# Sliced feed-forward on one core: the softmax over slices by sample halves, and half of the weight transposes moved

## What is computed

```python
fx_mid = (x @ W_fx + b_fx).reshape(B, N, H, D).transpose(0, 2, 1, 3)
x_mid = (x @ W_x + b_x).reshape(B, N, H, D).transpose(0, 2, 1, 3)
slice_weights = softmax((x_mid @ W_slice + b_slice) / temp, axis=-1)
slice_norm = slice_weights.sum(axis=2)
slice_token = einsum('bhnc,bhng->bhgc', fx_mid, slice_weights)
slice_token = slice_token / (slice_norm[..., None] + 1e-05)
q, k, v = slice_token @ W_q, slice_token @ W_k, slice_token @ W_v
attn = softmax(einsum('bhgc,bhkc->bhgk', q, k) * SCALE, axis=-1)
out_slice = einsum('bhgk,bhkc->bhgc', attn, v)
out_x = einsum('bhgc,bhng->bhnc', out_slice, slice_weights)
out_x.transpose(0, 2, 1, 3).reshape(B, N, INNER) @ W_out + b_out
```

## Time and profile before

| | us |
|---|---|
| median of 3 runs | 1218.9 |
| the runs | 1215.72, 1218.9, 1219.8 |
| the profiled execution | 1216.68 |
| its span | 1214.8 |
| mean granted TensorE clock | 0.977 of full speed |

### The profile page before, as it was taken

How to read it: one execution, slowest core, us unless ns; L and a number is a source line. 1 busy time by engine, 2 the same in 40 slices (tenths; PEclk the granted TensorE clock), 3 DMA queues, 4 the chain that set the end, 5 groups by cost and what they waited for, 6 DMA issues and landing times.

```text
span 1214.8 us, 43735 instructions
## 1 busy us (share of the span) xinstructions
PE 1131.3 (93%) x16184; PEld 787.9 (65%) x16184; DVE 856.7 (71%) x3021; ACT 752.9 (62%) x2435; POOL 617.1 (51%) x939
## 2 busy tenths in 40 slices
PE   6988979999999789999999997999999999999997
PEld 3447845555555467887788786777777764566765
DVE  5974679999999868787877775555555555766664
ACT  0126779999999745555555554566666666655453
POOL 6012568888888644555556554233333332345545
PEclk9988999999999999999999998999999999899999
DMA  7000000000000000000000000000000000000000
GB/s 239 1 1 1 3 2 1 0 0 0 0 0 0 2 2 3 0 0 0 0 0 0 0 1 2 2 0 0 0 0 0 0 1 1 1 11 11 17 17 19
DMA packets 10835, 10.26 MB, mean 8 GB/s; under 512 B 9233, under 2 KB 9873, under 8 KB 10641
## 3 DMA queue, kind: packets, MB, share of 16 engines
q1 hardware_dynamic: 10768, 9.35, 2.6%
HBM read 7.25 MB, written 2.10 MB: 8 GB/s over the span
## 4 chain that ended last, share of the span: by engine, by line
PE 65%; ACT 21%; DVE 6%; issue 5%; POOL 2%; DMA 0%; SPq 0%; ACTq 0%; POOLq 0%; DVEq 0%
ACT big L787 13%; PE bank L1473 8%; PE bank L1807 5%; PE bank L1155 5%; PE bank L1825 5%; PE bank L1468 5%; PE bank L1144 3%; PE bank L1456 3%; PE bank L1233 3%; PE bank L159 3%; PE bank L1164 3%; PE bank L1182 2%; PE bank L1586 2%; PE bank L1223 2%; PE bank L1203 2%
## 5 line engine op out<-in xcount | busy, mean ns | idle before, releaser
L787 ACT ACTIVATE big<-big 128x128 f32<-128x128 f32 x512 | 218.1, 645 | 0.5 <-DVE big L836 0.5
L787 ACT ACTIVATION_READ_ACCUMULATOR big<-big 128x1 f32 x512 | 181.5, 444 | 0.0
L620 POOL TENSOR_TENSOR big<-big 128x512 f32<-128x512 f32 x128 | 133.0, 1040 | 47.8 <-DVE big L825 47.6
L1058 POOL TENSOR_TENSOR big<-big 128x512 f32<-128x512 f32 x64 | 65.5, 1045 | 126.9 <-DVE big L1332 126.9
L1554 POOL TENSOR_TENSOR big<-g_a,g_b 64x64 f32 x128 | 40.1, 313 | 171.8 <-DVE g_a L1544 171.8
L836 DVE CUSTOM_DVE_ANT_0 big<-bank,cst 128x128 f32<-128x128 f32 x512 | 117.9, 287 | 2.3 <-issue 2.3
L1535 DVE TENSOR_TENSOR_SCAN g_t<-g_zero_r,bank 128x128 f32<-128x128 f32 x128 | 53.9, 421 | 87.0 <-ACT g_zero_r L1520 87.0
L738 PEld LDWEIGHTS bank<-cst,big 128*128 128x128 f32 x512 | 55.7, 141 | 68.9 <-POOL big L620 25.0
L1520 ACT ACTIVATE g_zero_r<-bank,g_bias 128x64 f32<-128x64 f32 x128 | 40.7, 318 | 90.0 <-PE bank L1473 89.9
L1868 ACT ACTIVATE big<-bank 128x512 f32<-128x512 f32 x128 | 66.0, 603 | 45.5 <-PE bank L1807 45.5
L1737 POOL TENSOR_TENSOR big<-big 128x512 f32<-128x512 f32 x48 | 60.9, 1269 | 63.6 <-DVE big L1944 61.0
(11 more groups left out here) (271 smaller groups left out, 3140.0 us busy)
## 6 DMA issues: line engine op xcount, KB each, us to landing
cst<-consts_dram SPq DMA_DIRECT2D x1, 3364.5 KB, 14.2
out_dram<-h SPq DMA_DIRECT2D x8, 256.0 KB, 2.6
big<-x_dram SPq DMA_DIRECT2D x3, 512.0 KB, 5.8
cst<-consts_dram SPq DMA_DIRECT2D x3, 256.0 KB
big<-x_dram SPq DMA_DIRECT2D x1, 513.0 KB, 4.2
big<-consts_dram SPq DMA_DIRECT2D x4, 96.0 KB, 2.2
cst<-consts_dram SPq DMA_DIRECT2D x4, 48.0 KB, 2.0
g_ih_exchanged<-consts_dram SPq DMA_DIRECT2D x2, 96.0 KB, 8.0
```

Source lines behind the costliest of these rows:

```text
L620: nc.gpsimd.tensor_tensor(P, P, a_rs[t % 4].unsqueeze(2).to_broadcast([128, 4, 128]), ALU.mult).then_inc(a_n_r, 1)
L787: m = nc.scalar.activation(P, P, ACT.Exp, bias=a_mx[tb % 4][:, k:k + 1], scale=-1.0, accum_out=a_sm[tb % 4][:, k:k + 1])
L1058: nc.gpsimd.tensor_tensor(w, w, f_rs[l][:, 8 * s:8 * s + 8].unsqueeze(2).to_broadcast([128, 8, 64]), ALU.mult).then_inc(f_w_r, 1)
```

## The change

The shift of the logits, the exponential, the sums and the reciprocals of pair a are done by sample halves of 512 columns (the maximum remains one instruction). The semaphores of these steps count two for each pair, and GpSimd waits for each half by itself. VectorE's order becomes: maximum and first half of the subtraction; normalizer and its reciprocal (`tokens_norm`); the addition of x into h; the scaling of the tokens; second half of the subtraction; variance or centring; first sum and reciprocal; `attended_scaled`; second sum and reciprocal. ScalarE does the second exponential between the copy of the transposed tokens and the copy of the second weights. TensorE does the first four weight transposes where all eight were, and the other four behind `tokensT`, ahead of `attended`. No matmul is added or removed.

```diff
--- before.py
+++ after.py
@@ -1051,9 +1051,8 @@
                                     one[:, 0:1].unsqueeze(1).to_broadcast([128, 2, 64]), ALU.add).then_inc(f_xs1_r, 1)
 
         def weights(i, l, n):
-            pool.wait_ge(f_rs_r, n)
-
             for s in range(2):
+                pool.wait_ge(f_rs_r, n * 2 + (s - 1))
                 w = f_w[l][:, 512 * s:512 * (s + 1)].rearrange("p (h g) -> p h g", g=64)
                 nc.gpsimd.tensor_tensor(w, w, f_rs[l][:, 8 * s:8 * s + 8].unsqueeze(2).to_broadcast([128, 8, 64]), ALU.mult).then_inc(f_w_r, 1)
 
@@ -1156,14 +1155,14 @@
                                      f_xs1[l][:, 96 * (k // 4):96 * (k // 4) + 96], start=True, stop=True)
             m.then_inc(f_s_r, 1)
 
-        def weightsT(i, l, n):
-            if l or exists(i, -1):
+        def weightsT(i, l, n, half):
+            if half == 0 and (l or exists(i, -1)):
 
                 pe.wait_ge(f_ls_r, n - 1)
-            for k in range(8):
-                m = nc.tensor.transpose(T(1, k // 4)[:, 128 * (k % 4):128 * (k % 4) + 128], f_w[l][:, 128 * k:128 * k + 128], eye)
-                if k % 4 == 3:
-                    m.then_inc(f_wt_r, 1)
+            for k in range(4):
+                at = 512 * half + 128 * k
+                m = nc.tensor.transpose(T(1, half)[:, 128 * k:128 * k + 128], f_w[l][:, at:at + 128], eye)
+            m.then_inc(f_wt_r, 1)
 
         def tokensT(i, l, n):
             pe.wait_ge(f_tk_r, n)
@@ -1185,7 +1184,7 @@
 
         def values(i, l, n, more):
             if more:
-                pe.wait_ge(f_sub_r, n + 1)
+                pe.wait_ge(f_sub_r, n * 2 + 2)
                 pe.sem_inc(f_go, 1)
             for s, h, j, p, q, r in PARTS3:
                 rows, cols = slice(64 * s, 64 * s + 64), slice(64 * h, 64 * h + 64)
@@ -1243,11 +1242,12 @@
             if exists(x[0], 0):
                 out(*x)
             if exists(z[0], 0):
-                weightsT(*z)
+                weightsT(*z, 0)
             if exists(y[0], 0):
                 pairsT(*y)
             if exists(z[0], 0):
                 tokensT(*z)
+                weightsT(*z, 1)
             if exists(y[0], 0):
                 if not exists(z[0], 0):
                     pe.wait_ge(f_tk_r, y[2])
@@ -1273,9 +1273,10 @@
             act.wait_ge(f_t_r, n)
             nc.scalar.activation(xT[l], bank[:, 128:256], ACT.Identity, bias=one[:, 0:1]).then_inc(f_xT_r, 1)
 
-        def exp(i, l, n):
-            act.wait_ge(f_sub_r, n)
-            nc.scalar.activation(f_w[l], f_w[l], ACT.Exp).then_inc(f_exp_r, 1)
+        def exp(i, l, n, s):
+            act.wait_ge(f_sub_r, n * 2 + (s - 1))
+            w = f_w[l][:, 512 * s:512 * s + 512]
+            nc.scalar.activation(w, w, ACT.Exp).then_inc(f_exp_r, 1)
 
         def weightsT(l, z, k):
             act.wait_ge(f_wt_r, z * 2 + (k - 1))
@@ -1289,7 +1290,7 @@
             if not l and exists(i, -2):
                 square(act, i + (LN[2] - 1), i * 4 - 8, 4, 0)
             if exists(a[0], 0):
-                exp(*a)
+                exp(*a, 0)
             if exists(zi, 0):
                 weightsT(zl, z, 0)
             if exists(yi, 0):
@@ -1298,6 +1299,9 @@
             if exists(zi, 0):
                 act.wait_ge(f_tt_r, z)
                 nc.scalar.copy(f_tT[zl], T(1, 2)).then_inc(f_tT_r, 1)
+            if exists(a[0], 0):
+                exp(*a, 1)
+            if exists(zi, 0):
                 weightsT(zl, z, 1)
                 act.wait_ge(f_u_r, z)
                 nc.scalar.copy(f_u[zl], T(1, 2)).then_inc(f_uc_r, 1)
@@ -1308,36 +1312,45 @@
         if start == 0:
             rowsT(0, 0, 1)
         elif start == 1:
-            exp(0, 0, 1)
+            exp(0, 0, 1, 0)
+            exp(0, 0, 1, 1)
         else:
             rowsT(0, 1, 2)
             pipelined3(act, slot)
 
     def stage3_dve(v, start=None):
-        def shifted(i, l, n):
+        def maxima(i, l, n):
 
             v.wait_ge(f_lg_r, n)
             lg = T(0, 0, 2).rearrange("p (h g) -> p h g", g=64)
             nc.vector.tensor_reduce(f_mx[l], lg, X, ALU.max).then_inc(f_mx_r, 1)
+
+        def shifted(i, l, n, s):
+
             v.wait_ge(f_mx_r, n)
-            nc.vector.tensor_tensor(f_w[l].rearrange("p (h g) -> p h g", g=64), lg, f_mx[l].unsqueeze(2).to_broadcast([128, 16, 64]),
-                                    ALU.subtract).then_inc(f_sub_r, 1)
-
-        def rsum(i, l, n):
-            v.wait_ge(f_exp_r, n)
-            nc.vector.tensor_reduce(f_rs[l], f_w[l].rearrange("p (h g) -> p h g", g=64), X, ALU.add).then_inc(f_sum_r, 1)
-
-        def rrsum(i, l, n):
-            v.wait_ge(f_sum_r, n)
-            nc.vector.reciprocal(f_rs[l], f_rs[l]).then_inc(f_rs_r, 1)
-
-        def tokens(i, l, n):
+            nc.vector.tensor_tensor(f_w[l][:, 512 * s:512 * s + 512].rearrange("p (h g) -> p h g", g=64),
+                                    T(0, s).rearrange("p (h g) -> p h g", g=64),
+                                    f_mx[l][:, 8 * s:8 * s + 8].unsqueeze(2).to_broadcast([128, 8, 64]), ALU.subtract).then_inc(f_sub_r, 1)
+
+        def rsum(i, l, n, s):
+            v.wait_ge(f_exp_r, n * 2 + (s - 1))
+            nc.vector.tensor_reduce(f_rs[l][:, 8 * s:8 * s + 8], f_w[l][:, 512 * s:512 * s + 512].rearrange("p (h g) -> p h g", g=64),
+                                    X, ALU.add).then_inc(f_sum_r, 1)
+
+        def rrsum(i, l, n, s):
+            v.wait_ge(f_sum_r, n * 2 + (s - 1))
+            nc.vector.reciprocal(f_rs[l][:, 8 * s:8 * s + 8], f_rs[l][:, 8 * s:8 * s + 8]).then_inc(f_rs_r, 1)
+
+        def tokens_norm(i, l, n):
 
             v.wait_ge(f_s_r, n + 2)
             nr = f_nr[l].rearrange("p (s j) -> p s j", s=2)
             nc.vector.tensor_scalar(nr, regions()[:, :, :, 64], 1e-5, None, ALU.add).then_inc(f_nr_r, 1)
             v.wait_ge(f_nr_r, n)
             nc.vector.reciprocal(f_nr[l], f_nr[l]).then_inc(f_nr2_r, 1)
+
+        def tokens(i, l, n):
+            nr = f_nr[l].rearrange("p (s j) -> p s j", s=2)
             v.wait_ge(f_nr2_r, n)
             nc.vector.tensor_tensor(f_tk[l].rearrange("p (j s c) -> p s j c", j=4, s=2), regions()[:, :, :, 0:64],
                                     nr.unsqueeze(3).to_broadcast([128, 2, 4, 64]), ALU.mult).then_inc(f_tk_r, 1)
@@ -1364,13 +1377,18 @@
             if exists(y[0], 0):
                 pairs_shifted(*y)
             if exists(a[0], 0):
-                shifted(*a)
+                maxima(*a)
+                shifted(*a, 0)
             if exists(z[0], 0):
-                tokens(*z)
+                tokens_norm(*z)
             if exists(xi, 0):
                 v.wait_ge(f_ot_r, x)
                 hp = h[:, bass.ds(xi * 4 + 2 * xl, 2), :]
                 nc.vector.tensor_tensor(hp, hp, T(1, 3)[:, 0:128].rearrange("p (b c) -> p b c", c=C), ALU.add).then_inc(f_h_r, 1)
+            if exists(z[0], 0):
+                tokens(*z)
+            if exists(a[0], 0):
+                shifted(*a, 1)
             if not l and exists(i, -2):
                 variance(v, i + (LN[2] - 1), i * 4 - 8, 4, 0)
             if l and exists(i, -1):
@@ -1378,15 +1396,21 @@
                 v.wait_ge(f_h_r, i * 2 + 2)
                 centre(v, i + LN[2], i * 4 - 4, 4, h)
             if exists(a[0], 0):
-                rsum(*a)
-                rrsum(*a)
+                rsum(*a, 0)
+                rrsum(*a, 0)
             if exists(y[0], 0):
                 attended_scaled(*y)
+            if exists(a[0], 0):
+                rsum(*a, 1)
+                rrsum(*a, 1)
         if start == 0:
-            shifted(0, 0, 1)
+            maxima(0, 0, 1)
+            for s in range(2):
+                shifted(0, 0, 1, s)
         elif start == 1:
-            rsum(0, 0, 1)
-            rrsum(0, 0, 1)
+            for s in range(2):
+                rsum(0, 0, 1, s)
+                rrsum(0, 0, 1, s)
         else:
             pipelined3(v, slot)
 
```

## The result

The changed kernel takes 1209.62 us (median; 1208.13 to 1211.1), the kernel before 1219.12 us beside it; the ratio is 0.9936, with a 95% interval of 0.9919 to 0.9954: 0.5 to 0.8% faster, about 7.8 us by this ratio (the two medians are 9.5 us apart). The profiled execution has a span of 1206.2 us, 8.6 less than the earlier trace rows.

What follows compares the result with a forecast made beforehand. TensorE, busy 93% of the span, was taken as the bound. Gains of 4.7 (loop), 1.2 (four slots outside), 0.65 (second slot) and 0.2 (start) make 6.7 us, forecasting 1211 us; range 1204 to 1219 us.

Steps and rivals of the forecast that it cites:

- What bounds the stage: In the changed stage, TensorE's own work and its few gaps set the end; TensorE busy 231.25 of 240.30 us.
- The ceiling drawn from it: Without removing matmuls, an edit here can win only 0.28 us a slot and perhaps a little slack in neighbouring groups.
- The gap's cause: Before the attended product: the 0.28 us gap comes from ScalarE's copy of the transposed pairs, 0.72 us with handovers.
- The term of 0.18 us a slot: Loop slots: from output product's end (zero) to attended product 2.14 us against 2.32, so 0.18 us gained each.
- Rival (a): Full cover: register step hidden or tokens ready in time; 0.30 to 0.41 us a slot, 1206 us; chance 0.15.
- Rival (b): On VectorE, tokens run in series behind the addition; gain 0.04 to 0.10 us a slot, 1214.5 us; chance 0.2.
- Rival (c): Nothing gained: the gap is the sequencer's and returns before the attended product; 1217 us; chance 0.05.
- Rival (d): Slower: the addition's wait on the output product holds tokens and TensorE longer; 1223 us; chance 0.07.
- The signs: Profile after: VectorE idle about 0.6 us a slot before the addition, no late start on pairs, no new slices wait.
- VectorE's extra instructions: Halved softmax steps on VectorE cost zero with its slack; skill-page estimate 0.25 us a slot, trace about 0.08.
- The four written-out slots: Four full slots outside the hardware loop gain 0.30 us each, 1.2 us together.
- The second slot: The stage's second slot, where TensorE waited 0.51 us for tokens, gains 0.65 us.

Runs made afterwards that it cites:

- e6: e3 with the output product in the transposed tokens' PSUM bank instead of the transposed pairs'; 1202.18 us (kernel before 1216.01), loop slot 9.187 us.
- e2: The changed kernel with all eight weight transposes back ahead of the pair transposes; 1212.55 us (kernel before 1215.66), loop slot 9.550 us.
- e9: The changed kernel with the loop's addition made to a fixed tile, its results not added into h; 1206.23 us (kernel before 1219.03), loop slot 9.370 us.
- e8: The changed kernel with the second half of the subtraction moved ahead of the tokens; 1227.66 us (kernel before 1216.01), loop slot 10.083 us.
- e3: The changed kernel with the scaling of the tokens back ahead of the addition into h; 1206.71 us (kernel before 1215.66), loop slot 9.352 us.
- e7: The kernel before with the moved weight transposes and e6's other bank, no halves, old VectorE order; 1205.78 us (kernel before 1216.01), slot 9.307 us.
- e1: The kernel before with only the second four weight transposes moved behind the token transposes; 1218.71 us (kernel before 1215.66), loop slot 9.761 us.
- e5: The changed kernel run again, unaltered, beside later experiments; 1208.28 us (kernel before 1216.01), loop slot 9.490 us.

## Why the prediction was right, step by step

**What bounds the stage** (TensorE's work and its few gaps) held: with busy time unchanged, the slot fell from 9.677 to 9.492 us, and the forecast was 9.49. The ceiling drawn from it did not hold. The prediction calls 0.28 us a slot, and perhaps a little slack, the whole of what an edit without fewer matmuls can win here; e6 removes no matmul and wins 0.49. Of that, 0.41 is the way from zero to the attended product, 1.91 us, which is the prediction's own figure for the stream alone, and 0.08 is the attended product, which takes 0.66 us in the stream and 0.74 behind a gap. Only 0.28 of the 0.49 us showed as the gap; the rest was hidden in the lengths of the groups.

**The gap's cause** (the copy of the transposed pairs, though the row said "issue") held. In e2, where the pair transposes run in the stream, the gap is 0.28 us again behind 0.44 us of token transposes: 0.72 us from their end, as was read from the earlier trace rows.

**The term of 0.18 us a slot** was measured at 0.185. Its pieces: addition 0.15 us after zero, measured 0.17; tokens 0.20 later, measured 0.20; tokens to the end of the token transposes 0.69 + 0.72, measured 1.41 (592.58 to 593.99); four weight transposes 0.44, measured 0.44; the credit for starting in the stream 0.06, measured 0.08 (the attended product's piece is 0.66 us against 0.74 in the earlier trace rows). The errors of 0.02 cancel, which is luck. The loop gave 4.8 us for 4.7.

**Rival (a)**, a hidden register step, is out: e9 puts the price at 0.12 us. **Rival (b)**, tokens in series behind the addition, is out: they start 0.20 us after it, 0.09 us before its recorded end. The Trainium skill's section on the DRAIN (VectorE: DVE Perf Modes) says itself that a next instruction that isn't held starts earlier, which the prediction left out; the rule without that exception, taken with recorded ends, doesn't describe this pair. **Rival (c)** is out: with the copy covered (it ends at 594.07 us) the changed kernel has no gap in front of the attended product (594.43 us), and e2 brings the gap back behind the copy. **Rival (d)** has the right mechanism and not the price: e8 shows that each 0.1 us ahead of tokens is 0.1 us a slot; its point of no gain (0.53 us from zero to tokens, measured 0.37 us) was not reached.

**The signs.** VectorE idles 0.74 us a slot before the addition, for about 0.6 forecast, with the output product as releaser; its idle time before the pairs fell from 1.42 to 0.48 us, so its start on them is not late. The slices show a releaser that the table of before doesn't name, GpSimd's weights (19.7 us of idle weight loading in 26 slots, where before it was 21.2 us of "issue"), but no new wait: the weights end at 588.56 us, the slices' loads start at 589.10 us, and the slices take 1.96 us in both chains.

**VectorE's extra instructions** cost it 0.26 us a slot and TensorE didn't notice: VectorE still idles in each slot before the pairs and now before the addition. The table of waits, 446 to 722 us, where L1362 is the maximum of the pairs (it answers to L1349 in the earlier trace rows):

```profile
DVE h L1387 <- PE bank L1232: 21.6, 29, 0.8
...
DVE big L1362 <- PE bank L1202: 13.8, 29, 1.4
...
PEld bank L1173 <- DVE big L1355: 2.3, 13, 0.2
```

The 0.26 us agree with the 0.25 us that was worked out from the Trainium skill (Perfetto Trace Analysis, Optimizing Scalar/DVE Operations); my own reading from one instruction, 0.08 us for the subtraction, was for that one alone, and I never summed the others. It changed nothing, because VectorE isn't saturated. The last row is the only one of this table that names tokens as a releaser; the prediction's "new gap of about 0.2 us before the token transposes" shows as 0.11 us of extra length in the chain.

**What I sized badly.** The stage as a whole gave 7.5 us, and 6.7 were forecast; the median is 1209.62 us, for 1211. The four written-out slots were put at 0.30 us each. Three of them gave 0.37 (without the pause's part), 0.47 and 0.36, the last one 0.2; why the first three gave more than 0.30, though the addition started 0.05 us after zero and not 0.03, I didn't take apart. The pause one slot ahead of the loop, 0.62 us of difference, was in no term. The second slot gave 0.57 for 0.65 and the start 0.14 for 0.2.

**What the prediction didn't ask.** It took the parts of the change as given and priced them. It says that the half subtraction frees VectorE 0.7 us before the addition, and didn't see that tokens would fit exactly there (e3), nor that the wait which forces the addition forward comes only from two results sharing a bank: the pair transposes overwrite what the addition has yet to read (e6, e7).

## What to carry to other kernels

When an engine is full but for a small wait, follow the releaser one step further before moving work into the wait: e1 filled the gap and lost 0.08 us a slot, since the next wait, for the addition, took its place. Where a wait exists because two results share a PSUM bank, try the other bank first: here that was worth 0.17 to 0.45 us a slot, and splitting the softmax 0 to 0.12. And order an in-order engine's queue by when each input arrives and who waits: what is ready before a wait should stand in front of it.

## What the runs showed of the hardware

The addition, whose address comes from the loop counter and which stands behind a wait on another engine, starts 0.17 us after that engine's end in the loop and 0.05 us after it with a fixed address (e9, and the written-out slots of the changed kernel). Its register step of 69 to 75 ns is executed when the wait is over: in e8's chain it starts at 592.27 us, behind the output product's end at 592.24, and the addition follows at 592.39. Where VectorE is still busy then, it costs nothing: in the kernel before it ran at 595.5 us, while tokens were being scaled.

A group of transposes that TensorE has to wait for costs more than the idle time that the profile shows: after 0.54 us of idle time in e8 four of them take 0.66 us from their start, and in the stream the chain gives four 0.44 us, because there the group starts 0.16 us ahead of the end of the one in front. Where the wait is short, only a longer group in the chain shows it.

TensorE's pause inside the pairs product, one slot ahead of the hardware loop, was 1.12 and 0.50 us in the profiles before and after, 0.78 us in e1 and 1.05 us in e6, and e5 shows none; what sets its length I didn't find out.
